# A sandwich of recurrent attention and mixture of experts: the first pass in another order of work

## What is computed

```
x = x + layernorm(attention(layernorm(x)))
# attention, per sequence (T = 512, C = 256)
xx = q_shift_1d(x)                       # a quarter of the channels from t-1, a quarter from t+1
k = (x*mix_k + xx*(1-mix_k)) @ Wk.T      # v and r alike
out[t] = (a + exp(u+k[t])*v[t]) / (b + exp(u+k[t]))
a = a*exp(w) + exp(k[t])*v[t];  b = b*exp(w) + exp(k[t])
attention = (sigmoid(r) * out) @ Wo.T
```

## Time and profile before

| | us |
|---|---|
| median of 3 runs | 1258.77 (1258.77 to 1259.7) |
| the profiled execution | 1250.62 |
| its span in the trace | 1248.8 |
| busy in the span: PE, DVE, POOL, ACT | 1012.4, 892.7, 844.3, 508.4 |
| share of the span: PE, DVE, POOL, ACT | 81%, 71%, 68%, 41% |

### The profile page before, as it was taken

How to read it: one execution, slowest core, us unless ns; L and a number is a source line. 1 busy time by engine, 2 the same in 40 slices (tenths; PEclk the granted TensorE clock), 3 DMA queues, 4 the chain that set the end, 5 groups by cost and what they waited for, 6 DMA issues and landing times. The chain is left out here.

```text
span 1248.8 us, 23009 instructions
## 1 busy us (share of the span) xinstructions
PE 1012.4 (81%) x6344; PEld 892.5 (71%) x6344; DVE 892.7 (71%) x2147; ACT 508.4 (41%) x885; POOL 844.3 (68%) x1047
## 2 busy tenths in 40 slices
PE   0557789889988998899889676778999999988553
PEld 0446578777777777687778566777999999988432
DVE  4677898779878877978797523456777667566496
ACT  3223433453445344534453233333444434333175
POOL 2244887887798779878887753145776667565498
PEclk9777999999999999999999779798999999899755
DMA  4232232443244224414532226579878898898586
GB/s 130 61 106 89 93 97 82 149 140 92 88 147 139 82 90 156 128 57 127 155 106 66 83 74 216 172 182 231 145 145 180 181 224 167 189 229 199 106 251 221
DMA packets 114548, 174.05 MB, mean 139 GB/s; under 512 B 13485, under 2 KB 93768, under 8 KB 112200
## 3 DMA queue, kind: packets, MB, share of 16 engines
q1 hardware_dynamic: 83304, 121.09, 32.5%
q0 software_dynamic: 26592, 35.67, 15.8%
q10 hardware_dynamic: 4608, 16.78, 3.6%
HBM read 173.53 MB, written 78.21 MB: 202 GB/s over the span
## 5 line engine op out<-in xcount | busy, mean ns | idle before, releaser
L1477 POOL DMA_INDIRECT sum_y<-e_y,e_row_at x142 | 222.7, 1569 | 42.9 <-issue 36.7
L1311 PE MATMUL e_h_ps<-e_z_hi,e_w 128*128 128x256 f32 x1136 | 223.5, 291 | 27.3 <-DMA e_w<-w_split 13.2
L1311 PEld LDWEIGHTS e_h_ps<-e_z_hi,e_w 128*128 128x128 f32 x1136 | 187.6, 198 | 29.7 <-issue 17.7
L1132 POOL DMA_INDIRECT slots_x<-f_xf,f_at x128 | 145.5, 1137 | 32.4 <-issue 32.1
L1311 PE MATMUL e_h_ps<-e_z_lo,e_w 128*128 128x256 f32 x568 | 163.9, 289 | 0.0
L1353 ACT ACTIVATE e_act_h<-e_h_ps,e_w 128x256 f32<-128x256 f32 x142 | 67.4, 475 | 201.9 <-PE e_h_ps L1311 201.9
L618 PE MATMUL f_h_ps<-f_f_hi,f_w_hi 128*128 128x512 f32 x256 | 109.1, 426 | 29.7 <-DVE f_h L900 25.8
L1327 PE MATMUL e_y_ps<-e_w,e_h_hi 128*128 128x256 f32 x568 | 118.4, 292 | 1.1 <-DVE e_h_lo L1399 1.1
L1392 DVE SCALAR_TENSOR_TENSOR e_h<-e_h_ps,e_w,e_act_h 128x256 f32<-128x256 f32 x142 | 68.1, 483 | 71.1 <-ACT e_act_h L1353 70.4
L1311 PEld LDWEIGHTS e_h_ps<-e_z_lo,e_w 128*128 128x128 f32 x568 | 112.1, 197 | 0.0
L862 DVE RECIPROCAL f_den<-f_den 128x256 f32<-128x256 f32 (+1 forms) x48 | 109.6, 2283 | 1.1
(11 more groups left out here) (227 smaller groups left out, 3038.9 us busy)
## 6 DMA issues: line engine op xcount, KB each, us to landing
e_w<-w_split SPq DMA_DIRECT2D x71, 1026.0 KB
e_w<-w_split ACTq DMA_DIRECT2D x71, 512.0 KB
e_x_in<-slots_x SPq DMA_DIRECT2D x71, 260.0 KB, 2.8
f_x_in<-x SPq DMA_DIRECT2D x16, 512.0 KB, 5.2
f_x_res<-x SPq DMA_DIRECT2D x16, 512.0 KB, 6.2
x_dram<-f_x SPq DMA_DIRECT2D x16, 512.0 KB, 7.0
sum_y<-f_y SPq DMA_DIRECT2D x32, 256.0 KB, 2.2
c_x<-x_dram SPq DMA_DIRECT2D x32, 256.0 KB
```

What stands on the lines that cost most here:

```text
L1132: pool.indirect_dma_start(out=slots_x[:, :], out_offset=bass.IndirectOffsetOnAxis(ap=at[p][:, j, k:k + 1], axis=0), in_=xf[p][:, j, :], in ...
L1311: last = pe.matmul(h_ps[q][:, which, :], w13(p, part)[:, which, c, q * P:(q + 1) * P], z[p % 2][:, c, :], start=(n == 0), stop=(n == 5))
L1477: pool.indirect_dma_start(out=dst[:, :], out_offset=bass.IndirectOffsetOnAxis(ap=row_at[p][:, j:j + 1], axis=0), in_=y[p][:, j, :], in_off ...
```

## The change

Four steps are moved.

1. On PE, `turn_xf` of c = 0 stood at the end of the iteration ahead of the next one's k, v, r. It now stands inside them, behind the 9 of the 27 matmuls of c = 0 that need only the unshifted first half of z. `f_high` and `f_low` of c = 0 move across the iteration's end with it: on ACT ahead of `exps`, behind `g_high(i, 1)` and `h_high(i - 3, 3)`; on DVE behind `product(i - 3, 3)`.
2. On DVE, the reciprocal of c = 0 is done in two halves of 256.
3. The three instructions that read the counts leave `place` and go between these halves, as `read_counts`.
4. On DVE, the product of q = 1 moves from behind `moments_x1` to right behind the second `scans`.

```diff
-            def kvr(s, c):
+            def kvr(s, c, chunks):
...
-                if c == 0:
+                if c == 0 and HERE in chunks:
                     pe.wait_ge(zhi_ready, s + 1)
                     pe.wait_ge(zlo_ready, s + 1)
-                wait(pe, exps_ready, 6 * s + 3 * c)
-                wait(pe, v_used, 2 * s + c)
+                if HERE in chunks:
+                    wait(pe, exps_ready, 6 * s + 3 * c)
+                    wait(pe, v_used, 2 * s + c)
...
+                    if part not in chunks:
+                        continue
...
-                last.then_inc(kvr_done, 1)
+                if SHIFT in chunks:
+                    last.then_inc(kvr_done, 1)
@@ PE
             def body(i, par):
-                kvr(i, 0)
+                kvr(i, 0, (HERE,))
+                turn_xf(i - 2, par, 0)
+                kvr(i, 0, (REST, SHIFT))
                 turn_xf(i - 2, par, 1)
                 project(i - 1)
                 route(i - 2, par)
-                kvr(i, 1)
+                kvr(i, 1, (HERE, REST, SHIFT))
...
                 inner(i - 2, par, 3)
-                turn_xf(i - 1, 1 - par, 0)
@@ ACT
                 h_high(i - 3, 3)
+                f_high(i - 2, par, 0)
                 exps(i, 0)
...
                 prepare(i, 1, ACT.Exp)
-                f_high(i - 1, 1 - par, 0)
                 g_high(i, 1)
@@ DVE
-                dve.wait_ge(rec_ready, 3 * s + n)
+                dve.wait_ge(rec_ready, 4 * s + n)
...
-            def place(s, p):
+            def read_counts(s):
...
                 dve.wait_ge(counted, s + 1)
                 dve.tensor_tensor(pos[:, :, :], rank_ps, by_rows(count, E), ALU.add).then_inc(placing, 1)
                 dve.wait_ge(prob_ready, s + 1)
                 dve.tensor_reduce(prob_sum[:, :], prob[:, :, :], mybir.AxisListType.X, ALU.add).then_inc(placing, 1)
                 dve.wait_ge(placing, s * PLACE_STEPS + 2)
                 dve.tensor_tensor(count[:, :], count[:, :], total_ps, ALU.add).then_inc(counts_read, 1)
...
                 product(i - 3, 3)
+                f_low(i - 2, par, 0)
                 moments_x(i + 1, 1 - par)
...
                 denominator(i, 0)
-                invert(i, 0, slice(0, T))
-                gate(i, 0, 1)
+                invert(i, 0, slice(0, T // 2))
+                read_counts(i - 2)
+                invert(i, 0, slice(T // 2, T))
+                gate(i, 0, 2)
                 place(i - 2, par)
                 normalise_o(i - 1, 1 - par)
                 product(i - 2, 0)
                 scans(i, 1)
+                product(i - 2, 1)
                 normalise_x(i + 1, 1 - par)
                 moments_x1(i - 1, 1 - par)
-                product(i - 2, 1)
                 denominator(i, 1)
...
                 invert(i, 1, slice(T // 2, T))
-                gate(i, 1, 3)
-                f_low(i - 1, 1 - par, 0)
+                gate(i, 1, 4)
```

More of the change, by code:

```diff
@@ L941, in rank_experts @@
                     .then_inc(mask_ready, 1)
+            def read_counts(s):
+                if not inside(s, SEQS):
+                    return
+                dve.wait_ge(counted, s + 1)
+                dve.tensor_tensor(pos[:, :, :], rank_ps, by_rows(count, E), ALU.add).then_inc(placing, 1)
+                dve.wait_ge(prob_ready, s + 1)
+                dve.tensor_reduce(prob_sum[:, :], prob[:, :, :], mybir.AxisListType.X, ALU.add).then_inc(placing, 1)
+                dve.wait_ge(placing, s * PLACE_STEPS + 2)
+                dve.tensor_tensor(count[:, :], count[:, :], total_ps, ALU.add).then_inc(counts_read, 1)
             def place(s, p):
@@ L951, in then @@
                     dve.wait_ge(placing, s * PLACE_STEPS + n)
[L953 to L958, removed]
                 dve.tensor_tensor(picked[:, :, :, :], chosen[:, :, :, :],
```

## The result

The changed kernel takes 1265.03 us (median of 11 executions, 1261.71 to 1268.62). The kernel before, beside it on the same chip, takes 1257.53. The ratio is 1.0056, with an interval of [1.0037, 1.0076]: slower by 0.56%, or 7 us. The forecast was 1244.3, faster by 1.15%, with a range of 1237 to 1258. Both the sign and the range were wrong. Each time in the table of the experiments is the median of a kernel's fast executions; one slow execution of e2 (1290.44 us) and one of e8 (5385.12 us, for a reason that stays open) are left out.

A forecast was written before the change was run, and what follows sets the result against it. The prediction took one dependency chain through PE, ACT, DVE and POOL, tied with POOL's own ring, as the bound. Periods -18.6, ramp -2, tail +1.1, clock +5 gave -14.5: 1258.77 to 1244.3 us, range 1237 to 1258.

The forecast's parts named there:

- Product q=1 behind the scans: On DVE, the product moved before normalising and moments: PE's 1.24 us stop goes, nothing changes on the period's critical path.
- the chain: Dependent work through each period, from k,v,r over ACT, DVE and POOL to z_lo, claimed without slack except 1.82 us at its end.
- DVE's wait of 1.53 us: DVE's one wait between f_lo and z_lo, at 307.26, for POOL's sum f_den; the moved product stays ahead of it.
- Rival (2): POOL's ring stretches by a second send, or by DVE's ranking instructions beside POOL's sums: 6 or 12 us; chance 0.15.
- Period, chain A: Quiet period of the first pass after the change: 41.98 - 1.70 + 0.41 + 0.15 = 40.84 us.
- The 0.15 us that I charged for the cut: DVE's reciprocal of c = 0 in two halves costs 3.50 us, 0.15 more than whole, in each period.
- PE's stop at L622 for q = 3: PE's wait for product q=2 before the q=3 matmuls (L618 before) grows from 0.49 to some 2.3 us.
- rival (4): xf or f_lo of c=0 misses its 0.9 or 0.6 us margin, stopping PE within k,v,r: 1257 to 1261; chance 0.06.
- The clock: Lower granted PE clock after longer stops: 5 us, a quarter of the upper bound of 1.54 in 13 periods, 20 us.
- rival 1: PE's stop at q=3 brings 1.2 GHz in nearly each period: 20 us replaces 5, about 1259 to 1262; chance 0.11.
- The ramp: Start of the first pass, with the longest stop for xf, 5.8 us: 2 us saved, bounds 1 and 3.
- The tail: Last two sequences, with no k,v,r to cover the transposes, pay 0.56 and a copy of 0.58: 1.1 us.

The follow-up runs named there:

- e2: Kernel before with only the product of q = 1 moved behind the second scans: 1278.43 us, ratio 1.0174.
- e8: Kernel before with only the xf transposes moved and POOL's sums of c = 0 put ahead of two of the four sends: 1235.36 us, ratio 0.9841.
- e10: Changed kernel with only POOL's sums of c = 0 put ahead of two of the four sends: 1258.76 us, ratio 1.0.
- e7: Changed kernel with the product of q = 1 back behind moments_x1 and POOL's sums of c = 0 ahead of two of four sends: 1236.2 us, ratio 0.9849.
- e4: Changed kernel with one wait added: POOL starts its sums of c = 1 only when f_xn is ready: 1248.64 us, ratio 0.9938.
- e1: Changed kernel with only the product of q = 1 put back behind moments_x1: 1247.1 us, ratio 0.993.
- e5: Kernel before with only the xf transposes moved, and f_hi and f_lo of c = 0 with them: 1245.03 us, ratio 0.9924.
- e6: Kernel before with only the reciprocal cut in halves and the counts read between them: 1256.86 us, ratio 1.0011.
- e9: Changed kernel with the product of q = 1 between normalise_x and moments_x1, POOL's sums of c = 0 ahead of two sends: 1234.84 us, ratio 0.9812.

## Why the prediction was wrong

**What failed.** The step is "Product q=1 behind the scans", with its words "DVE does the same work before its wait at 307.26, so the chain doesn't see it". The work is the same and its duration is not. I took a duration from one place of the trace for an instruction that the edit moved to another, 0.65 us later, beside other work of POOL. The sum then had 0 for this term; e10 against e7 measures +25 us, and the changed kernel against e4, with the same clock in both, 16.7. The cover that I named, DVE's wait of 1.53 us, was there and was used up, 1.35 us short.

The evidence stood in the trace of before: 4.20 us at 55.10 and 3.25 at 91.42 for an instruction group that takes 1.36 in every steady period. Two other DVE instructions were stretched beside POOL in each steady period (the rows stand at "Which instructions are hit"), and the prediction took them at their stretched length, since they stayed in place. Its sentence on contention spoke of instructions with two SBUF inputs; f_xn has one, and so stood outside it. I had looked for stretched instructions on POOL (the sends), not on DVE.

**Rival (2)** had the right kind of thing, DVE's small ranking instructions beside POOL's sums. It put 6 to 12 us on it; f_below measures 0.88 more per period in e1, 13 x 0.88 = 11.4, where e5 against e8 gives 9.7 and e1 against e7 10.9. In the changed kernel it strikes in 6 of 13 periods, about 5 us. But the rival named only the ranking and the sends, and so none of my cases had f_xn in it.

**What held.** The xf transposes left the chain, worth 1.70 less 0.41 by the sum: e7's steady periods are the 40.84 of "Period, chain A". That this fits so closely is partly luck, as e7 also has another order on POOL, and e8, for which the same sum without the cut gives 40.69, has 40.9 to 41.0. The halves of the reciprocal take 1.75 and the counts buy nothing (e6). The 0.15 us that I charged for the cut doesn't show there. PE's stop at L622 for q = 3, which I put at 2.3 us, is 1.77 in the changed kernel, where PE already stops for f_xn; in e4, where it doesn't, PE's row reads:

```profile
265.21 0.51 PE L622 MATMUL f_h_ps<-f_f_hi,f_w_hi 128*128 128x512 f32 x1 [2.30 <-DVE f_h L905]
```

The margins of xf and f_lo, rival (4), were kept: no steady period has a wait for them inside k, v, r.

**The clock** (5 us, rival 1) can't be told from the rest in one number. In the changed kernel 13 periods are 29.0 us longer than 13 x 40.84. The holds are 13 x 1.35 = 17.6 and 6 x 0.88 = 5.3, which leaves 6.1 us for the clock and for the first period, which is long in every kernel (44.04 here, 42.70 in e7). One period took 44.89 at 0.92, where the other steady ones with a short f_below take 42.3 to 42.9. PE stops twice in each, for instance 1.73 us for f_xn at 309.66 and 1.77 for q = 3 at 313.92; between 311 and 317 us the granted clock was 0.76.

The forecast meant the stop for q = 3, and e4 has it without the one for f_xn: it ends at 307.14 and is 2.38 us long. Behind it:

```profile
305.00:311.00 6.00, 3.86 (x10) 3.09 (x11) 5.97 (x6) 2.81 (x6) 5.69 (x9) 0.72 0.78 248
```

From sequence 3 to 15 the clock is 0.98 in e4 and 0.98 in the changed kernel. In e1 and e7 the product is back, the stop for q = 3 is 0.5 us, and the clock is 1.00. So the mechanism of the forecast was right. Its price is less sure: e4's 13 periods are 2.7 us longer than e1's, although f_below is long in 7 of them and not in 12. At 0.88 each that makes up to 7 us, and the 5 lies between. The reason for taking a quarter was misread: the two slow periods of the kernel before followed stops of 1.59 us, not 1.7 and more, and longer ones, up to 1.89, brought nothing.

**The ends of the pass.** The ramp gave 2.8 us (103.25 to 100.47) for my 2. The tail, from the first k, v, r matmul of sequence 15 to the experts' first transposes, was 132.98 us and is 136.98: 4.0 for my 1.1. In the experiments it is 1.1 to 4.0 over before where xf is moved, and 1.4 and 2.2 in e2 and e6, where it isn't, so that not all of it can be laid to xf. The experts' pass, in which no instruction is changed, was 5.9 us longer in this profile (463.6 to 469.5). It varies between kernels by several us (460.5 in e5, 471.0 in e9), and why stays open.

In sum, against the 1236.1 us that the forecast gave the profiled execution: the periods +29.5 (43.07 for 40.8), the clock's term already in them -5, ramp -0.8, tail +2.9, experts +5.9: 32.5, and it took 1268.6.

## What to carry to other kernels

A duration belongs to a place as much as to an instruction. Before you move a DVE instruction, list the min, median and max of its group over the whole trace; where the max is several times the median, find what POOL did beside it, and price the new place by that row. And where POOL runs work back to back, ask what on DVE reads two SBUF tensors, or reads and writes SBUF in a plain scale and shift, within that stretch: here 2.5 us of sums made one 0.40 us instruction 3.28, and another, 0.60 beside the second sum alone, 1.47. The remedies that paid were on POOL's side: one wait at no cost (e4), and an idle engine at the right moment (e7's 2.22 us) rather than a full one.

## What the runs showed of the hardware

**One DVE instruction waits out several of POOL.** The fourth f_xn, 0.40 us alone, ended at 309.6 behind two sums and part of a send. f_below in e1 ended with the second sum, though the first ended 1.25 us earlier. Without POOL's sums beside it, at the end of the pass, f_below takes 0.19 us. DVE got no turn between the two sums. In the ramp it did. There, in the kernel before, POOL began its sums at 55.26 out of an idle wait, and of the four f_xn behind 55.10 the last three took one POOL instruction each:

```profile
L813 DVE TENSOR_SCALAR f_xn<-f_x_in,f_mean,f_rstd x4: 385/1348/1352, 55.1 to 57.9; 128x256 f32<-128x256 f32 x4
```

The Trainium skill (SBUF — State Buffer, SBUF: two separate sides) says that DVE and GpSimd share a port pair that one of them holds exclusively, "for the whole instruction", and that the other blocks. The trace agrees with the block, and in the ramp with its length; in the steady loop the block outlasts one POOL instruction. When DVE gets a turn and when not stays open.

**The hold begins ahead of the sum.** In the changed kernel the fourth f_xn starts 0.4 us into the second send (306.3 against 305.95) and is held. In e4 it starts as far in (300.7 against 300.36) and isn't:

```profile
L818 DVE TENSOR_SCALAR f_xn<-f_x_in,f_mean,f_rstd x4: 399/400/401, 299.8 to 300.7; 128x256 f32<-128x256 f32 x4
```

The only difference on POOL is that in e4 the sum behind the send must wait for f_xn. So the send alone doesn't hold this instruction. A sum that is queued with nothing to wait for seems to take effect before it shows as begun (306.94): by 0.2 us at least, since the instruction would have ended at 306.7, and by 0.6 if it was held from its start. How it does that, no run here shows, and the profile's times on POOL are rough.

**Which instructions are hit.** f_xn goes from SBUF to SBUF and f_below reads SBUF twice. Two more that read SBUF twice are stretched in every steady period of the kernel before: the scan of b_sum is 1.22 us for c = 0, and 1.79 to 2.04 for c = 1, beside POOL's add of x (297.88 to 300.30); the gate's product f_g is 0.69 for c = 0, and 1.48 to 1.51 for c = 1, beside POOL's g_lo (from 313.66). Beside the same add, f_ekv, with one input in PSUM, is as short as for c = 0, where it is 0.68 too:

```profile
282.82 1.22 DVE L842 TENSOR_TENSOR_SCAN f_b_sum<-f_ew,f_ek 128x512 f32<-128x512 f32 x1
...
298.14 0.68 DVE L839 TENSOR_TENSOR f_ekv<-f_ek,f_v_ps 128x512 f32<-128x512 f32 x1
...
299.33 2.04 DVE L842 TENSOR_TENSOR_SCAN f_b_sum<-f_ew,f_ek 128x512 f32<-128x512 f32 x1
...
314.01 1.49 DVE L870 TENSOR_TENSOR f_g<-f_num,f_den 128x512 f32<-128x512 f32 x1
```

Not every instruction from SBUF is hit: the moments of x1 (f_stats, one SBUF input) take 0.40 to 0.41 us beside the sums. f_on, the same operation as f_xn from PSUM, is no test here: in the kernel before POOL stands idle and waits for it. By the Trainium skill (VectorE: DVE Perf Modes, "Mode 2×_2P — use both read ports for one tensor") such a scale and shift from SBUF in fp32 uses both read ports, and one from PSUM doesn't. The rows agree in that f_xn is shorter than f_on (0.40 and 0.53 us for 256 columns), but no experiment here changed where an operand lies, and no run shows the ports.

**What single stops of PE cost in clock.** In e7, PE's longest stop is 1.5 us in each period, and from 225 to 592 us the granted clock is 1.00 without a break:

```profile
225.00:592.00 367.00, 341.21 (x1899) 283.60 (x1899) 314.93 (x684) 165.24 (x279) 309.04 (x432) 1.00 0.38 119
```

With a longest stop of 1.8 us in each period (e9) two periods in 12 fall to 0.97, and with one of 2.3 (e4) the clock drops in seven places. The kernel before stops for xf once in each period, 1.4 to 1.9 us, and two of these, both of 1.59, were followed by a drop. So a single stop of 1.5 us cost nothing here, and one of 2.3 did. e10 has a stop of 1.72 us that ends at 310.63 and one of 1.77 that ends at 314.89, and such a pair in each period; its periods alternate between 42.0 and 43.3 us over most of the pass. From 359.19, where one of the long ones starts, to 370 the granted clock was 0.89.
